# Mamba block with a sparse expert layer: scan decays in a ring of four, half of it in SBUF, and one tile in five that ends a unit later

## The reference, cut to what matters

```python
xn = layernorm(x)
x  = x + mamba(xn) + moe(xn)
# mamba: the part that the change touches
delta = softplus(dt_raw @ dt_proj_w.T + dt_proj_b)
dA  = exp(einsum('bti,is->btis', delta, A))        # the decays
dBu = einsum('bti,bts->btis', delta * u, B_ssm)
h   = dA_t * h + dBu_t                             # for each t in order
y_t = einsum('bis,bs->bi', h, C_t)
...
y = (ys + u * D_param) * silu(z)
return y @ out_proj_w.T + residual
# moe, for each token and its two experts
act = silu(x @ w1.T) * (x @ w3.T);  out = sum of weight * (act @ w2.T)
```

## Time and profile before

| | us |
|---|---|
| median of three runs | 2660.86 (2654.14 to 2668.02) |
| the profiled execution | 2653.93 |
| its span, first to last instruction | 2652.2 |
| DVE busy in the span | 2459.2 |
| PE busy | 2292.8 |
| POOL busy | 2031.0 |
| ACT busy | 1658.9 |
| mean granted clock of PE | 0.936 |

### The profile page before, as it was taken

The page is one execution under the profiler, slowest core; times in us unless marked ns, Lnnn a source line. Parts: engine busy times, 40 slices in busy tenths (PEclk is TensorE's granted clock), DMA queues, the critical chain, the costliest instruction groups (busy, mean ns, idle before and its releaser), DMA issues. The chain is left out here.

```text
span 2652.2 us, 47132 instructions
## 1 busy us (share of the span) xinstructions
PE 2292.8 (86%) x14442; PEld 1986.7 (75%) x14442; DVE 2459.2 (93%) x4041; ACT 1658.9 (63%) x4137; POOL 2031.0 (77%) x1607
## 2 busy tenths in 40 slices
PE   3958789899999999998999989999989899998665
PEld 2855578878787887877888877888877787887554
DVE  7679999999999999999999999999999999999997
ACT  3940566666666666666666666666666666666653
POOL 3430678888888888888888888888888888888883
PEclk7858899999999999999999999999999999999776
DMA  7216045565555555555555555555555555542451
GB/s 244 92 40 216 29 124 156 154 176 152 161 151 152 157 160 171 158 157 153 155 160 155 166 163 151 158 156 160 154 162 164 156 152 157 159 113 52 96 100 32
DMA packets 267099, 379.38 MB, mean 143 GB/s; under 512 B 21492, under 2 KB 158324, under 8 KB 266852
## 3 DMA queue, kind: packets, MB, share of 16 engines
q1 hardware_dynamic: 236196, 332.26, 40.2%
q0 software_dynamic: 28480, 43.94, 10.1%
q10 hardware_dynamic: 2176, 0.18, 0.1%
HBM read 332.59 MB, written 52.10 MB: 145 GB/s over the span
## 5 line engine op out<-in xcount | busy, mean ns | idle before, releaser
L475 POOL TENSOR_TENSOR h<-du,bbc 128x512 f32<-128x512 f32 x1024 | 1362.5, 1354 | 505.3 <-PE HT L1305 375.3
L1071 DVE TENSOR_TENSOR_SCAN h<-DA,carry,h 128x256 f32<-128x256 f32 x2048 | 1417.7, 734 | 91.4 <-ACT DA L748 79.0
L748 ACT ACTIVATE DA<-delta,alog 128x256 f32<-128x256 f32 x2048 | 882.6, 468 | 212.2 <-DVE h L1071 200.9
L1305 PE MATMUL HT<-ident,h 128*128 128x128 f32 x4096 | 665.8, 288 | 260.5 <-DVE yT L1082 259.1
L1305 PEld LDWEIGHTS HT<-ident,h 128*128 128x128 f32 x4096 | 496.6, 148 | 416.2 <-issue 375.2
L1082 DVE SCALAR_TENSOR_TENSOR yT<-HT,cT,yT 128x512 f32<-128x512 f32 x960 | 698.5, 728 | 3.1 <-PE HT L1305 3.1
L1354 PE MATMUL G<-xtT,W 128*128 128x128 f32 x2160 | 273.2, 281 | 0.0
L1368 PE MATMUL G<-W,fill 128*128 128x256 f32 x1080 | 271.8, 397 | 0.0
L1361 PE MATMUL G<-xtT,W 128*128 128x128 f32 x2160 | 263.4, 275 | 0.0
L1354 PEld LDWEIGHTS G<-xtT,W 128*128 128x128 f32 x2160 | 261.1, 198 | 0.0
L1361 PEld LDWEIGHTS G<-xtT,W 128*128 128x128 f32 x2160 | 252.2, 192 | 0.0
(11 more groups left out here) (183 smaller groups left out, 2986.6 us busy)
## 6 DMA issues: line engine op xcount, KB each, us to landing
W<-in_w_T_dram SPq DMA_DIRECT2D x405, 512.0 KB, 4.2
bbc<-b_dram SPq DMA_DIRECT2D x256, 256.0 KB, 4.3
xraw<-in_x_dram SPq DMA_DIRECT2D x64, 256.0 KB, 2.7
xn_dram<-W SPq DMA_DIRECT2D x8, 1032.0 KB, 14.0
W<-in_x_dram SPq DMA_DIRECT2D x32, 256.0 KB, 6.7
moe_dram<-fill SPq DMA_DIRECT2D x32, 256.0 KB, 4.0
out_dram<-tmpA SPq DMA_DIRECT2D x32, 256.0 KB, 2.2
out_dram<-moe_dram POOLq DMA_DIRECT2D x32, 256.0 KB, 4.4
```

The source lines that it names most:

```text
L475: pool.tensor_tensor(h[:, v % RING], du[:, b, 2 * q:2 * q + 2, :], bbc[:, s // 2 % BRING, s % 2, :].unsqueeze(1).to_broadcast([P, 2, T]), ...
L748: i = act.activation(DA[:, v % 2, k, :], delta[:, b, c, :], ACT.Exp, scale=nega[:, c, s:s + 1])
L1071: i = dve.tensor_tensor_scan(h[:, v % RING, k, :], DA[:, v % 2, k, :], h[:, v % RING, k, :], carry[:, b, s, c:c + 1], ALU.mult, ALU.add)
L1305: i = pe.transpose(HT[:, k, c * P:(c + 1) * P], h[:, (2 * s + c // 2) % RING, c % 2, k * P:(k + 1) * P], ident[:, :])
```

## The change

The ring of decays has four slots from block 2 on. Slots 0 and 1 are the two of `DA` in PSUM; slots 2 and 3 are `decay_sb`, a view of `scratch[4]` in SBUF. `decay(g)` gives the place for unit g, `decay_user(g)` the unit that used it last. ACT makes the decay of unit g + 3 in unit g, where it made that of g + 1. In blocks 0 and 1 all is as before. Units 2 and 3 of every four thus have their decay in SBUF, and their scans read two tensors from SBUF.

For the first of the five tiles of a block the second multiply (`MULT`), Y and the scaling (`YO`) stand one unit later; the others keep theirs. The scatter of every tile stands one unit later. The second half of the x projection, `xs1`, stands one unit earlier.

```diff
+        decay_sb = scratch[4].rearrange("p (r c t) -> p r c t", r=2, c=2)
...
+        DECAY_AHEAD = 3
+        def decay(g):
+            slot = g % 4 if g >= 2 * U else g % 2
+            return DA[:, slot] if slot < 2 else decay_sb[:, slot - 2]
+        def decay_user(g):
+            if g >= 2 * U + 4:
+                return g - 4
+            return g - 2 if g < 2 * U + 2 else -1
...
-                at = U * (k // len(XT_UNITS)) + XT_UNITS[k % len(XT_UNITS)] + stage
+                at = U * (k // len(XT_UNITS)) + XT_UNITS[k % len(XT_UNITS)]
+                at += stage[k % len(XT_UNITS)] if isinstance(stage, tuple) else stage
...
-                 ... "xs1": 10, ...
+                 ... "xs1": 9, ...
...
-        XT, XT_COPY, H1, H3, TANH, A2, MULT, Y, YO, SCATTER = 0, 1, 2, 3, 3, 4, 4, 5, 6, 8
+        XT, XT_COPY, H1, H3, TANH, A2, SCATTER = 0, 1, 2, 3, 3, 4, 9
+        MULT, Y, YO = (5, 4, 4, 4, 4), (6, 5, 5, 5, 5), (7, 6, 6, 6, 6)
...
-                wait(act, s_scan, 32 * n + v - 1)
+                g = 32 * n + v
+                wait(act, s_scan, decay_user(g) + 1)
-                    i = act.activation(DA[:, v % 2, k, :], delta[:, b, c, :], ACT.Exp, scale=nega[:, c, s:s + 1])
+                    i = act.activation(decay(g)[:, k, :], delta[:, b, c, :], ACT.Exp, scale=nega[:, c, s:s + 1])
...
-                    if v < 31:
-                        make_da((j, b), v + 1)
-                    elif nxt:
-                        make_da(nxt, 0)
+                    g = unit(j, b, v)
+                    for to in range(made, min(g + (1 if g < 2 * U - 1 else DECAY_AHEAD), 2 * JB * U - 1) + 1):
+                        blk = to // U
+                        make_da((blk // 2, blk % 2), to % U)
+                        made = to + 1
...
-                    i = dve.tensor_tensor_scan(h[:, v % RING, k, :], DA[:, v % 2, k, :], h[:, v % RING, k, :],
+                    i = dve.tensor_tensor_scan(h[:, v % RING, k, :], decay(g)[:, k, :], h[:, v % RING, k, :],
```

More of the change, by code:

```diff
@@ L789, in _ @@
             make_da((0, 0), 0)
+            made = 1
             act.wait_ge(s_stats, LATE_MOMENTS + NEWTON + FINISH)
@@ L794, in step @@
             def step(j, b):
+                nonlocal made
                 nxt = after(j, b)
```

## The result

| | before | changed |
|---|---|---|
| median, us | 2660.61 (4 runs, 2654.14 to 2668.02) | 3188.36 (4 runs, 3183.7 to 3190.88) |
| profiled execution, us | 2653.9, span 2652.2 | 3183.7, span 3182.0 |
| a block, from block 2 on, us | 76.4 | 94.1 |
| idle of DVE in a block, us | 3.75 | 1.85 |

The ratio of the times is 1.1975 (95% interval 1.1938 to 1.2012): the changed kernel is 20% slower.

A forecast was written before the change was run, and what follows sets the result against it. DVE was taken to set the time; 17 us a block of blocked scans less 3.4 us of gaps gave +13.6 us x 30 = +408 us on 2652.2 us, forecast as 3065 us, range 2700 to 3250.

The forecast's parts named there:

- the wait that the second buffer was to remove: DVE's waits for ACT's decays, from block 2 on: all 43.9 us should go, 1.5 us a block.

The follow-up runs named there:

- e8_swapped: The changed kernel with units 0 and 1 of every four reading their decay from SBUF, units 2 and 3 from PSUM; 3120.69 us.
- e3: The changed kernel with the tiles' gathers and scatters issued by SP as plain DMAs, taken off POOL; 2954.28 us.
- e6: The changed kernel with decays made one unit ahead instead of three, the ring of four kept; 3221.3 us.
- e7: The changed kernel with a ring of three, two slots in PSUM and one in SBUF, decays made two units ahead; 2994.68 us.
- e12: The changed kernel with tile stages, scatter and xs1 put back as before, only the ring of four left; 3073.79 us, ratio 1.1547.

## What to carry to other kernels

Before an operand of a DVE instruction moves from PSUM to SBUF, look whether its other input is in SBUF too, and lay POOL's reading instructions over it: here each such scan paid 0.64 us on average, and the wait that the second buffer was to remove was worth 1.5 us a block against 17. If a second buffer is wanted, use it in the few units where POOL is idle: two units in 32 cost 0.2 to 0.4 us a block. And when a DMA moves by one place on POOL, look at what it then stands in front of, even if it has time to spare.

## What the runs showed of the hardware

- Between back-to-back POOL multiplies a waiting scan with two SBUF inputs gets in at each boundary, one for one (3.13 us for two scans beside 2.88 us for two multiplies).
- Behind a DMA that POOL itself issues it may not: the first scans took 5.2 and 6.1 us in block 17, behind a scatter and three or four multiplies, and 10.45 us at most, at a plain DMA. With the tiles' DMAs on another queue these scans went from 79 to 6. The DMA can stand several instructions ahead (unit 25 of e8_swapped), as long as POOL has worked without a break since. Counted over the traces of the changed kernel and of e3, e6, e7, e8 and e12: of 1859 held-up scans with no DMA in POOL's unbroken rows before them none was passed over at a boundary between two rows of POOL; of 632 with one, 303 were.
- POOL's next row starts 0.54 us before the row of a scatter ends (1754.08 against 1754.62). That overlap isn't needed for the long wait, since the gather of e12_ring_only at 1697.65 has none. What the cause is stays open, and why only about half of the scans behind a DMA are passed over.
- A fill by POOL that only writes SBUF held up no scan: 213 scans that overlap such fills alone have a mean of 731 ns and take 750 at most.
- An Exp of 256 columns takes 31 ns longer with SBUF as its output than with PSUM (499 against 468 ns).
